# Convolution-kernel rows: four column positions in PSUM, and their stores issued by ScalarE

## The reference, cut to what matters

```python
K = 2.0 * jnp.einsum('hn,hnl->hl', Cs, jnp.exp(P)).real     # 64 channels x 1024 taps
y = irfft(rfft(u * mask) * rfft(K))[..., :L] + u * mask * D  # causal convolution, skip term D
probs = softmax(y @ gate_w.T); vals, idx = top_k(probs, 2)   # 2 of 16 experts for each row
x = x + sum_over_e(w[e] * (silu(y @ g[e].T) * (y @ u[e].T)) @ d[e].T)
```

## Time and profile before

| | |
|---|---|
| median of 3 runs | 488.37 us (484.63 to 492.79) |
| profiled execution, its own time | 489.8 us |
| its span, first to last instruction | 488.0 us |
| TensorE busy | 435.9 us, 89% of the span |
| VectorE, ScalarE, GpSimd busy | 195.4, 107.9, 168.8 us |
| mean granted TensorE clock | 0.978 |
| moved by DMA | 115.99 MB, 238 GB/s |
| convolution stage | from 33.3 us to about 212 us of the span |

### The profile page before, as it was taken

How to read it: one execution, slowest core, us unless ns; L and a number is a source line. 1 busy time by engine, 2 the same in 40 slices (tenths; PEclk the granted TensorE clock), 3 DMA queues, 4 the chain that set the end, 5 groups by cost and what they waited for, 6 DMA issues and landing times.

```text
span 488.0 us, 9071 instructions
## 1 busy us (share of the span) xinstructions
PE 435.9 (89%) x2822; PEld 375.5 (77%) x2822; DVE 195.4 (40%) x525; ACT 107.9 (22%) x257; POOL 168.8 (35%) x213
## 2 busy tenths in 40 slices
PE   0379999999999998987899999999799999999991
PEld 0369999998989998965777888887578788887770
DVE  6932444443344434488333333332322233333330
ACT  3980010000000000071022222221222232222220
POOL 4643223322222110001772443344244663453322
PEclk9987999999999999998999999999999999999996
DMA  8977978989989998896799988978898996777650
GB/s 275 339 229 224 273 256 239 283 274 276 280 283 294 304 311 265 277 336 242 253 326 260 238 241 252 306 159 220 247 249 208 218 275 147 163 161 121 108 80 14
DMA packets 46491, 115.99 MB, mean 238 GB/s; under 512 B 10098, under 2 KB 25714, under 8 KB 46322
## 3 DMA queue, kind: packets, MB, share of 16 engines
q1 hardware_dynamic: 25138, 73.49, 47.1%
q0 software_dynamic: 12096, 33.58, 30.8%
q10 hardware_dynamic: 9216, 8.39, 5.4%
HBM read 93.63 MB, written 40.66 MB: 275 GB/s over the span
## 4 chain that ended last, share of the span: by engine, by line
PE 47%; DMA 32%; DVE 7%; issue 5%; SPq 3%; POOLq 2%; POOL 1%; ACT 1%; DVEq 0%; ACTq 0%
PE conv_ps L1058 20%; DMA out<-arena,from_row 19%; PE conv_ps L1207 12%; DMA k_rows<-k_sb 9%; PE conv_ps L1226 7%; DMA arena<-k_rows 3%; PE turn_ps L1216 3%; PE conv_ps L1165 2%; POOLq L473 2%; SPq L336 1%; POOL out L479 1%; DVE tmp L667 1%; PE turn_ps L1069 1%; SPq L335 1%; ACT arena L580 1%
## 5 line engine op out<-in xcount | busy, mean ns | idle before, releaser
L1058 PE MATMUL conv_ps<-arena 128*128 128x256 f32 (+7 forms) x1024 | 159.8, 314 | 7.6 <-DMA arena<-k_rows 7.6
L1058 PEld LDWEIGHTS conv_ps<-arena 128*128 128x128 f32 x1024 | 151.5, 196 | 15.8 <-issue 7.0
L1207 PE MATMUL conv_ps<-arena,ys_t 128*128 x640 | 127.8, 353 | 1.9 <-DVE ys_t L1005 1.9
L1207 PEld LDWEIGHTS conv_ps<-arena,ys_t 128*128 128x128 f32 x640 | 118.1, 191 | 13.5 <-issue 13.5
L479 POOL DMA_INDIRECT out<-arena,from_row x40 | 62.8, 1571 | 125.4 <-DMA out<-arena,from_row 77.1
L1226 PE MATMUL conv_ps<-arena,hid_t 112*128 x160 | 76.0, 597 | 5.2 <-DVE hid_t L1020 5.2
L772 DVE TENSOR_TENSOR arena<-conv_ps,mask_t 128x256 f32<-128x256 f32 x64 | 27.1, 424 | 91.9 <-PE conv_ps L1058 91.0
L1025 DVE TENSOR_SCALAR arena<-conv_ps,slot_weight 128x512 f32<-128x512 f32 x40 | 30.0, 751 | 70.4 <-DMA out<-arena,from_row 40.0
L1226 PEld LDWEIGHTS conv_ps<-arena,hid_t 112*128 112x128 f32 x160 | 27.3, 190 | 26.2 <-issue 26.1
L627 ACT ACTIVATE arena<-conv_ps,slot_weight 128x512 f32<-128x512 f32 x40 | 27.5, 687 | 76.2 <-DMA out<-arena,from_row 42.1
L1013 DVE TENSOR_TENSOR hid<-silu,conv_ps 128x112 f32<-128x112 f32 x40 | 10.8, 271 | 82.0 <-ACT silu L621 82.0
(11 more groups left out here) (177 smaller groups left out, 343.2 us busy)
## 6 DMA issues: line engine op xcount, KB each, us to landing
arena<-k_rows SPq DMA_DIRECT2D x64, 512.0 KB, 6.4
arena<-gu_t SPq DMA_DIRECT2D x16, 896.0 KB, 9.1
y_rows<-y_blk ACTq DMA_DIRECT2D x64, 128.0 KB, 4.5
arena<-x_time SPq DMA_DIRECT2D x56, 128.0 KB, 5.3
arena<-d_t SPq DMA_DIRECT2D x16, 448.0 KB, 11.2
arena<-x_time SPq DMA_DIRECT2D x2, 512.0 KB, 5.9
out<-arena,from_row POOLq DMA_INDIRECT x44, 7.0
out<-ys SPq DMA_DIRECT2D x1, 512.0 KB, 7.4
```

What stands on the lines that cost most here:

```text
L1058: last = nc.tensor.matmul(conv_ps[:, h, d * B:C * B], toep[:, p, h, d * P:(d + 1) * P], u_t[:, p, h, 0:(C - d) * B], start=(d == 0), stop= ...
L1207: last = nc.tensor.matmul(gu_ps, ys_t[:, t % 2, c, :], flat[:, bass.ds(bufs[t] * WE + c * GU, GU)], start=(c == 0), stop=(c == C - 1))
```

## The change

The four products of a group go to four column positions of TensorE, so that channel h stands on partitions 32h to 32h+31 of the PSUM bank, in 32 columns. `k_sb` follows (128 partitions, 32 elements). The skip term is loaded as a column for each group, zero but for four partitions, and added to column 0 of all 128 partitions. The rows are stored by four DMAs instead of one. They are issued in ScalarE's queue, at places of its own order; SP keeps only the wait for them (64 instead of 16).

```diff
-        skip_row = sb("skip_row", [1, H])
+        skip_col = sb("skip_col", [P, G])
-        k_sb = sb("k_sb", [LO, 2, HG, LO])
+        k_sb = sb("k_sb", [P, 2, LO])
-        k_ps = k_bank[0:LO, 0:HG * LO].rearrange("p (h n) -> p h n", h=HG)
+        k_ps = k_bank[:, 0:LO]
...
-            sp.dma_start(skip_row[:, :], skip).then_inc(par_in, 16)
+            sp.dma_start(skip_col[:, :], skip).then_inc(par_in, 16)
...
-            sp.wait_ge(pads_out, 16)
...
-                sp.wait_ge(k_added, g + 1)
-                sp.dma_start(bass.AP(k_rows, g * HG * KROW + P - 1, [[LO, LO], [KROW, HG], [1, LO]]),
-                             k_sb[:, p, :, :]).then_inc(k_stored[p], 16)
-
-                sp.wait_ge(k_stored[p], 16 * (i + 1))
+                sp.wait_ge(k_stored[p], 64 * (i + 1))
...
+            def kernel_out(g, p):
+
+                act.wait_ge(k_added, g + 1)
+                for h in range(HG):
+                    act.dma_start(bass.AP(k_rows, (g * HG + h) * KROW + P - 1, [[LO, LO], [1, LO]]),
+                                  k_sb[h * LO:(h + 1) * LO, p, :]).then_inc(k_stored[p], 16)
...
             waves(1, 1, True)
+            act.wait_ge(pads_out, 16)
+            kernel_out(0, 0)
             growth(10 * HG, H)
-            for g in range(2, 5):
-                waves(g, g % 2, False)
+            waves(2, 0, False)
+            kernel_out(1, 1)
+            waves(3, 1, False)
+            kernel_out(2, 0)
+            waves(4, 0, False)
             for p in range(2):
+                if p == 1:
+                    kernel_out(3, 1)
                 rows_out(p, p)
                 partials(p, p, True)
                 waves(5 + p, 1 - p, False)
             with act.Fori(1, (G - 6) // 2) as i:
                 for p in range(2):
+                    kernel_out(2 * i + p + 2, p)
                     rows_out(2 * i + p, p)
                     partials(2 * i + p, p, False)
                     waves(2 * i + 5 + p, 1 - p, False)
...
             for g in range(G - 6, G - 1):
+                if g + 2 < G:
+                    kernel_out(g + 2, g % 2)
                 rows_out(g, g % 2)
...
-                    dve.wait_ge(k_stored[p], 16 * i)
-                nc.vector.tensor_copy(k_sb[:, p, :, :], k_ps[:, :, :]).then_inc(k_copied, 1)
+                    dve.wait_ge(k_stored[p], 64 * i)
+                nc.vector.tensor_copy(k_sb[:, p, :], k_ps).then_inc(k_copied, 1)
                 dve.wait_ge(k_copied, g + 1)
-                nc.vector.tensor_tensor(k_sb[0:1, p, :, 0], k_sb[0:1, p, :, 0], skip_row[0:1, hs(g)],
+                nc.vector.tensor_tensor(k_sb[:, p, 0:1], k_sb[:, p, 0:1], skip_col[:, bass.ds(g, 1)],
                                         ALU.add).then_inc(k_added, 1)
...
-                    last = nc.tensor.matmul(k_ps[:, h, :], am[:, p, h, :], bm[:, p, h, :], start=True, stop=True)
+                    last = nc.tensor.matmul(k_ps[h * LO:(h + 1) * LO, :], am[:, p, h, :], bm[:, p, h, :],
+                                            start=True, stop=True)
```

More of the change, by code:

```diff
@@ L1272 @@
                                     c[:, :, 0].T, c[:, :, 1].T], axis=1), (2, 1, 1)),
-        "skip": np.asarray(L0_cond_D).reshape(1, H),
+        "skip": np.pad(np.asarray(L0_cond_D).reshape(G, HG, 1), ((0, 0), (0, 0), (0, LO - 1))).reshape(G, P).T,
         "gate_t": np.pad(np.asarray(L0_ffn_gate_w).reshape(E, C, P).transpose(2, 1, 0), ((0, 0), (0, 0), (0, Q - E))),
```

## The result

The changed kernel takes 501.33 us in the median of 4 runs (498.4 to 504.79); beside them the kernel before took 486.5. The ratio is 1.0298 (95% interval 1.0245 to 1.035): slower by 14.5 us (14.8 between the medians). The profiled execution took 501.91 us, its span is 500.0, against 489.8 and 488.0 before.

The account below looks back on a forecast made before the run. Bound: TensorE's convolution and the experts' accumulating stores. Start 1.2 + 0.3, six pairs of 23.4, two groups of 10.66 put group 15 9.6 us later (9.3 with products): 499.1, plus 2 for clock, 501.1; median about 500, range 488 to 517.

Parts of the forecast that it names:

- ScalarE's order: ScalarE's queue: the store of group g+2 stands behind `waves` of g+4, first issue 3.69 us after group g's convolution.
- This is the step that decides.: Moving the store into ScalarE's order: half of the rows' 18 us lead is given away, in every group.
- The sum of the path: Group g's end to group g+2's start: 3.69 + 1.4 issues + 2.8 landing + 4.96 to restart + 0.3 = 13.15 us.
- My 0.3 us for it: SP's loads: y_rows stores, pushed back by four issues, overlap the first load more; 0.3 us, between nothing and 0.9.
- a chain over the odd groups: Convolution loop: stalls of about 2 us in every second group, 1 to 13, six pairs of 23.4 us.
- the pace without waits: Convolution loop: group follows group by 10.66 us where no load is late, so at most 4.4 us can be won.
- The start: Before group 1: store 0's four issues delay the exponentials before `waves` 2, 1.2 us; skip column load 0.3 us.
- TensorE's clock: Convolution loop: stalls of 2.1 us may drop TensorE to 1.2 GHz; one fall of six counted, 2 us.
- rival 1: Convolution loop: the clock falls in most stalls, six times 1 to 4 us, total 504 to 522 us; chance 0.15.
- Rival 2: Stores land no sooner on ScalarE's queue than on SP's, 6.9 not 2.8 us: about 522 to 525 us; chance 0.08.
- Rival 3: Convolution loop: the store path is shorter than TensorE's pace, total 484 to 492 us; chance 0.22.
- Rival 4: TensorE's products: the four positions give no overlap, which moves the time by 0.3 us; within every case, no separate chance.

Follow-up runs that it names:

- experiment 4: Changed kernel with ScalarE issuing the four stores ahead of `waves`, a group earlier, instead of behind it: 482.36 us, ratio 0.9903 to the kernel before.
- experiment 2: Kernel before in layout, its one store moved from SP to the changed kernel's places in ScalarE's queue: 486.51 us, ratio 1.0025.
- experiment 1: Changed kernel with the four stores issued by SP, before the loads of their group: 497.57 us, ratio 1.0217 to the kernel before.
- experiment 5: Kernel before with one store behind `waves` on ScalarE, plus an idle ScalarE copy ahead of each store of groups 3 to 15: 493.38 us, ratio 1.012.
- experiment 6: Kernel before in layout, its one store issued by ScalarE between `partials` and `waves`: 478.86 us, ratio 0.984.
- experiment 7: Group 0's four stores issued by SP, in two kernels: stores ahead of `waves`, 477.65 us, ratio 0.9814; changed kernel, 497.70 us, ratio 1.023.
- experiment 8: Changed kernel with the six early copies of x issued behind the first expert loads instead of in the start: 509.1 us.

## Why the prediction was right, and where it was not

**The direction and the size** came out: 500 forecast, 501.33 measured; TensorE's wait for the loads 17 forecast, 17.5 measured. That both are so close is partly luck. Group 15 started 13.7 us later and not 11.3 (9.3, and 2 for the clock), and 1.6 us came back by chance behind it. Within the 13.7, the start and the clock cost 2.2 and 1.3 us more than forecast, and the rest of the loop 1.1 less. Of the wait, 2.5 us more stood before group 0, and less in the loop.

**ScalarE's order.** Right, and shown: the stores were issued within 0.5 us of the start of each wave, and moving them ahead of the waves removed every stall (experiment 4).

**"This is the step that decides."** Named too broadly. The late place has no slack, but by itself it costs nothing, since its pair of 21.97 us equals the old cycle's (experiment 2). What costs is each issue added to that path (experiments 1, 5, 6). My own sum held this, 23.4 - 1.4 against 2 x 10.97, and I did not read it off.

**The sum of the path.** From the end of group g to the start of g+2: 13.15 forecast, 13.7 in the turn shown. Over the eight turns that ended in a wait it was 11.7 to 14.6 and 13.1 in the mean, so the sum was right, and its parts missed both ways. The first store left after 3.8 us in the mean (3.69 forecast). From there to SP's first issue it was 3.7 and not 4.2, since the store landed in 1.5 to 3.1 us, by turns, where I had 2.8. The loads came later: TensorE started 4.5 to 6.7 us after SP's first issue, 5.7 in the mean, instead of 4.96. The chain of the changed kernel shows the loads:

```profile
81.07 5.67 DMA arena<-k_rows
...
106.09 5.38 DMA arena<-k_rows
...
153.86 4.77 DMA arena<-k_rows
...
177.60 6.24 DMA arena<-k_rows
```

The y_rows stores, pushed back by the four issues, are then under way; that they are the cause is only argued. My 0.3 us for it was too small by 0.4.

**Which groups.** I forecast a chain over the odd groups. TensorE waited before 3, 4, 6, 7, 8, 9, 10 and 12. From group 2 at 62.04 to group 12 at 183.89 are five pairs of 24.4 us; the odd ones took (194.3 - 51.6) / 6 = 23.8, and 24.1 without their first pair. Both chains have the same path and either can lead. No stall stood before 14 and 15, as forecast. The loop lost 10.0 us; the forecast had 8.1, and 2 more for the clock, which took 3.3. And the pace without waits was read too high: groups 1 to 6 of the kernel before follow each other by 10.60 us and not 10.66, so 5.2 us could have been won there, not 4.4.

**The start.** The term that was mis-sized: 1.5 us forecast, 3.7 measured. Of the copies of x I had only said that store 0 would no longer share a ring with them. It did not share the ring and was held all the same (experiments 7 and 8). The four issues did not cost 1.9 us there but 5.5.

**TensorE's clock.** I counted one fall of six, rival 1 had all. Two were seen. Windows of the changed kernel, columns as in the earlier trace rows:

```profile
86.00:90.00 4.00, 3.13 (x11) 2.96 (x12) 1.69 (x6) 0.52 (x1) 1.63 (x4) 0.66 1.03 399
158.00:162.00 4.00, 3.24 (x11) 3.00 (x12) 2.27 (x7) 0.52 (x1) 1.13 (x3) 0.62 1.01 358
183.00:187.00 4.00, 3.11 (x33) 2.82 (x34) 2.10 (x7) 0.52 (x1) 1.73 (x5) 1.00 1.03 381
```

After 2.46 us idle and after 1.76 us the first channel ran at 1.2 GHz for most of its time and took 4.15 us instead of 2.48, 1.7 us each; after 2.45 us idle at 183.89 the clock stayed at 2.4. So six falls are refuted, and the two cost 3.3 us, inside the loop's 10, where I had 2.

**Rival 2**, landing on ScalarE's queue as late as on SP's, is refuted for the place of the change: 2.7 us in the median of 64 stores, against 6.9. But it is the moment and not the queue that makes the difference. In the changed kernel the last of SP's eight loads had been issued 4 us or more before the store (at 144.93 and 149.10 us in the turn shown). In the early order, where ScalarE's stores leave while SP issues its loads or shortly after, they landed in 5.6 us (experiment 4) and 7.0 us (experiment 6), as late as SP's own, 5.8 (experiment 1) and 6.9. So the prediction's reason for SP's late stores, that they lie behind the loads in one ring, is not borne out, and its other reading, by the age of the loads, is. The Trainium skill, "DMA: Bandwidth & Descriptors", section "Issuing engines are not separate DMA queues", says that the DMAs of all issuing engines run on the same 16 engines and interleave, and that another issuing engine saves only the time of issuing; the 5.6 and 7.0 us beside 5.8 and 6.9 agree. **Rival 3** failed with the path of 13 us; its 484 is what the early order reaches and passes. (Its bound in the prediction is a slip: 499.1 less six times 1.1 is 492.5, not 491.6.) **Rival 4**: the positions do save, 0.17 us a group, which the stalls swallow.

## What to carry to other kernels

Before moving a DMA to another engine's queue, find what it will stand behind there and when that is released, then add up the path to its consumer and back; the free place is ahead of the wait in which the engine idles anyway. Don't expect it to land sooner for being on another queue: look at what else is under way at that moment. In a path without slack, count each DMA issue at 0.45 to 0.5 us: four small stores for one cost 2 to 3% here, and the number was a worse choice than the engine. The start is a place of its own: one issue behind large copies held ScalarE for 4.11 us. When a sum says that one part of a change costs nothing, write that down, since it says which part to undo.

## What the runs showed of the hardware

- Large copies from DRAM to DRAM issued by SP held small stores on ScalarE's own queue: 5.0 us to land instead of 1.4, and the next issue blocked ScalarE itself for 4.11 us. Without the copies it was 0.44.
- How late a small store landed went with what was under way and not with its queue: on ScalarE's it took 2.7 us (median) 4 us or more behind SP's last load and 5.6 to 7.0 among SP's loads, on SP's 5.8 to 6.9.
- A granted clock of 1.2 GHz followed idle stretches of 1.76 and 2.46 us and not one of 2.45 us, so the length of one stretch does not decide it.
- Eight products of 128x32 took 0.44 us on one column position and 0.27 on four.
